# The norm between the second tree and the second graph layer waits for its gathered rows tile by tile

## What is computed

```python
x = x + _L0_ffn_ref(_layernorm(x, axis=-1)[None], ...)[0]   # ends with: return y + _fff(y, f_nw, ..., gelu)
xn = _layernorm(x, axis=-1)
x = x + _L1_gnn_ref(xn, edge_index, L1_gnn_W, L1_gnn_b) + _L1_mix_ref(xn[None], ...)[0]
```

## Time and profile before

| | |
|---|---|
| three runs | 2998.49, 2992.94 and 2996.53 us, median 2996.53 us |
| the profiled execution, its own time | 2996.26 us |
| the span that its trace covers | 2994.4 us |
| PE busy | 2788.4 us, 93% of the span |
| DVE, POOL, ACT busy | 1264.0, 790.9 and 582.8 us |

### The profile page before, as it was taken

One profiled execution on the slowest core, in us unless ns is written; L12 is line 12 of the kernel. 1 busy time (PEld: TensorE's weight loads), 2 busy tenths in 40 slices (PEclk: granted clock), 3 DMA queues, 4 the chain that ended last, 5 costly groups with the idle time before them and its releaser, 6 DMA issues.

```text
span 2994.4 us, 44272 instructions
## 1 busy us (share of the span) xinstructions
PE 2788.4 (93%) x15119; PEld 2273.6 (76%) x15120; DVE 1264.0 (42%) x1884; ACT 582.8 (19%) x784; POOL 790.9 (26%) x585
## 2 busy tenths in 40 slices
PE   7999999999999999989899999989969999888998
PEld 5679977799999999886667766667658879876444
DVE  8515699463323333374444434232443115233422
ACT  2222245321121221210111011101012212121110
POOL 0777699143322223221310001000013223310000
PEclk9999999999999999999899999989979999989999
DMA  5222212312211111330798988116931211111675
GB/s 201 64 79 72 61 53 89 89 49 68 67 44 53 43 43 57 128 146 35 267 346 293 335 279 312 52 54 220 318 110 36 72 62 50 57 51 44 212 250 196
DMA packets 104522, 378.54 MB, mean 126 GB/s; under 512 B 17672, under 2 KB 18353, under 8 KB 102965
## 3 DMA queue, kind: packets, MB, share of 16 engines
q1 hardware_dynamic: 83520, 301.25, 28.9%
q0 software_dynamic: 18560, 56.97, 6.3%
q10 hardware_dynamic: 2294, 18.27, 1.6%
HBM read 344.51 MB, written 31.75 MB: 126 GB/s over the span
## 4 chain that ended last, share of the span: by engine, by line
PE 76%; DVE 8%; issue 7%; DVEq 5%; DMA 2%; ACT 2%; POOL 0%; ACTq 0%; SPq 0%
PE pair L890 74%; DVE big L2226 2%; DVEq L2213 2%; PE pair L935 1%; DVE asum L2375 1%; ACT big L1625 1%; DVEq L2242 1%; DMA ring<-in_tree_w 1%; DMA ring<-in_wts 0%; DVEq L2076 0%; PE pair L1047 0%; DVE big L1927 0%; DVE rstd L2077 0%; DVE mu L2077 0%; DMA big<-xn_spill 0%
## 5 line engine op out<-in xcount | busy, mean ns | idle before, releaser
L890 PEld LDWEIGHTS pair<-big,ring 128*128 128x128 f32 x3200 | 451.9, 194 | 148.5 <-issue 81.8
L890 PE MATMUL pair<-big,ring 128*128 (+1 forms) x3200 | 539.2, 321 | 22.5 <-issue 10.0
L890 PE MATMUL pair<-mean_high,low 128*128 128x314 f32 x1280 | 290.8, 309 | 0.0
L890 PE MATMUL pair<-ring,hid_plan_heads 128*125 128x512 f32 x576 | 275.2, 601 | 14.9 <-DVE big L2226 14.3
L703 POOL DMA_INDIRECT edge_records<-big x160 | 208.9, 1305 | 110.3 <-issue 58.8
L890 PEld LDWEIGHTS pair<-mean_high,low 128*128 128x128 f32 x1280 | 215.0, 191 | 0.0
L744 POOL TENSOR_TENSOR low<-ring,high_tmp_a 128x1024 fp32r<-128x1024 f32 x36 | 97.0, 2695 | 428.6 <-ACT high_tmp_a L1705 428.6
L2226 DVE TENSOR_TENSOR big<-pair,big 125x1024 f32 x144 | 176.2, 1223 | 28.9 <-PE pair L890 20.7
L890 PE MATMUL pair<-ring,big 128*128 128x512 f32 x384 | 172.8, 606 | 8.2 <-DVE big L2792 8.2
L890 PE MATMUL pair<-big 125*128 125x128 f32 (+9 forms) x830 | 158.0, 344 | 13.2 <-ACT big L1515 2.6
L890 PEld LDWEIGHTS pair<-ring,hid_plan_heads 128*125 128x125 f32 x576 | 96.7, 188 | 93.8 <-issue 70.2
(11 more groups left out here) (488 smaller groups left out, 4826.2 us busy)
## 6 DMA issues: line engine op xcount, KB each, us to landing
ring<-in_tree_w SPq DMA_DIRECT2D x288, 512.0 KB
ring<-in_wts SPq DMA_DIRECT2D x276, 512.0 KB
counts_spill<-big POOLq DMA_DIRECT2D x1, 5349.1 KB, 29.0
big<-in_x_rows SPq DMA_DIRECT2D x5, 512.0 KB, 8.8
xn_rows_spill<-big POOLq DMA_DIRECT2D x1, 2560.0 KB, 8.5
edge_records<-big POOLq DMA_INDIRECT x160
big<-xn_rows_spill POOLq DMA_DIRECT2D x1, 2560.0 KB, 10.7
sorted_out_q<-big POOLq DMA_DIRECT2D x5, 512.0 KB, 5.6
```

The source lines that it names most:

```text
L890: ins = pe.matmul(o, lhsT, rhs, start=start, stop=stop)
```

## The change

The f tree's gathers no longer share a semaphore: each tile has its own, `tile_back[t]`. The wait at the head of the norm is now for the five stores (`out_stored["f"]`), and in the loop over tiles the addition of tile t waits for the gather of tile t alone.

```diff
-        rows_back = {f: sem(f"rows_back_{f}") for f in "qkvf"}
+        rows_back = {f: sem(f"rows_back_{f}") for f in "qkv"}
+        tile_back = [sem(f"tile_back{t}") for t in range(NT)]
...
-                    ).then_inc(rows_back[f], 16)
+                    ).then_inc(tile_back[t] if f == "f" else rows_back[f], 16)
...
                 if name == "ln2":
-                    v.wait_ge(rows_back["f"], 16 * NT)
+                    v.wait_ge(out_stored["f"], 16 * NT)
...
                     if name == "ln2":
+                        v.wait_ge(tile_back[t], 16)
                         j = JOB[f"ln2_in{t}"]
                         v.tensor_tensor(rows(t), ps[SLOT[j]][0:T, :], tok(b)[:, t, :],
                                         ALU.add).then_inc(psum_free[SLOT[j]], 1)
```

## The result

The changed kernel takes 2989.44 us, the median of 20 runs (2984.32 to 2997.22), beside 2995.52 us for the kernel before, 20 runs as well (2989.37 to 3003.24). That is 6.08 us less; the ratio is 0.998 with a 95% interval of 0.9972 to 0.9989. A second series of the same kernel, on another chip, gave 0.9984 (0.9974 to 0.9994); two of its twelve executions, 3305.37 and 7581.14 us, were far slower than the rest and are left out of its figures. So it is faster, by about as much as the forecast, 7.2 us, or a little less.

A forecast was written before the change was run, and what follows sets the result against it. PE was taken as the bound, busy 93% of the span, with an exposed gather wait before the norm. 7.31 us less 0.1 gave 7.2 us off 2996.53, so 2989.3 us; range 2985.5 to 2993.8 us.

The forecast's parts named there:

- The exposed wait and its size: Before the norm, DVE idles 11.08 us for the last gather; starting on tile 0 brings its first addition 7.31 us forward.
- What the start hangs on: Norm's first addition starts once tile 0 has landed, read from packets as 2191.1 to 2191.25 us; start taken as 2191.45.
- The signs: Expected in the changed trace: first addition 4.1 to 4.5 us after POOL's first gather, aggregation 24.9 us after it, not 32.1.
- the prediction's own limit of 6 us: Forecast counts as wrong if the stretch from first gather to the aggregation's first matmul shrinks by less than 6 us.
- Padding and POOL: Padding's 0.30 us leaves the path; DVE's earlier work beside POOL's gathers costs 0 to 0.3 us, taken as 0.1.
- Later tiles: In the norm, tiles 1 to 4 land before their additions, tile 1 almost 1 us early; cost taken as 0.
- The rival of a lagging DMA engine: Tile 1 lands late and holds the norm's second addition up to 0.8 us; gain 6.4 to 7.2 us; chance 10%.
- the other estimate: Skill's formula for a GpSimd-issued DMA: tile 0 lands 3.2 us after issue, gain about 8.3 us; not adopted.
- late clock: PE's clock rises late at the aggregation, 3.2 us at half speed; 1.6 us less gain, 2990.9 us; chance 10%.
- Slower than before: Behind the norm, over four of some eight slow-clock stretches last twice as long, erasing the gain; 2997.8 us; chance 5%.
- no effect: Tiles do not land one by one or DVE's start stays tied to all five gathers; 2996.5 us; chance 5%.
- The bound of 0.2%: Whole kernel: a measurement tells 0.2%, 6.0 us, from no change; faster 65%, within 31%, slower 4%.

The follow-up runs named there:

- padding late: Changed kernel, but the norm's padding waits for tile 0's gather instead of the stores; 2988.17 us beside 2997.58 us for the kernel before, ratio 0.997.
- added work of two SBUF inputs: Changed kernel plus four unused DVE additions with both inputs in SBUF, behind the residual's additions, beside POOL's gathers; one execution, 2988.84 us.
- residual early: Changed kernel with six of the eight residual additions moved ahead into the tree's last three steps; 2989.00 us beside 2996.46 us before, ratio 0.9976.
- added work of one SBUF input: Changed kernel plus one unused 4.07 us DVE reciprocal with a single SBUF input, behind the residual's additions, beside POOL's gathers; one execution, 2984.62 us.
- PE filled: Changed kernel with PE turning each of the first three tiles back three times in the norm; 2990.16 us beside 2996.46 us before, ratio 0.9978.

## Why the prediction was right, and where it was off

**The exposed wait and its size.** Right. The shift of the first addition was put at 7.31 us less 0.1; 7.20 us were measured (17.32 to 10.12), and 7.15 us at the aggregation. Counting sixteen small packets as the landing of a tile held: sixteen of them stand just ahead of the first addition here too.

**What the start hangs on.** Missed, and the sum did not need it. The sum took tile 0's landing from the packets of the trace and is right whatever held the gather. The signs took it from the start of POOL's first gather: the addition was to come 4.1 to 4.5 us behind it, and it was 5.21 us; from that gather to the aggregation 25.82 us were measured, not 24.9. In the profile of before, the stores landed 5.22 us after the last was issued, so the gather was held by the residual's additions for less than 0.1 us (1.03 us, beside 0.99 to 1.01 us where nothing held the first gather). In other executions the stores land sooner, the gather starts sooner, and the hold makes up the difference. So its start is a poor mark to count from: in the second series the stretch from the first gather to the aggregation is 26.51 us, 5.6 us less than before, and by the prediction's own limit of 6 us the forecast would have been wrong there, although the gain counted from the last tree addition is 7.02 us. Its other sign, a span that does not shrink, did appear in the profile, and came from the tree's later end. The rows showed this kind of hold; I looked for it at the padding and the norm, and not at the instructions that were already there.

**Padding and POOL.** The padding was put at 0.30 us; with the padding late it takes 0.29 us of the path. The 0.1 us that the prediction took off for POOL beside DVE's new work did not show: the padding ran beside a gather that the residual's additions held anyway, and the four later gathers took 0.94 to 0.98 us, as before.

**Later tiles.** Right: tile 1 is there 0.8 us ahead of its use (the prediction had almost 1 us), and additions 1 to 4 keep their pace. The rival of a lagging DMA engine, and with it the 6.5 us that I derived from the remark on two slower engines in the Trainium skill ("DMA: Bandwidth & Descriptors", Latency and other measured facts), did not come about: tile 1 was 2.4 us behind tile 0. Nor did the other estimate, a landing 3.2 us behind the issue and a gain of 8.3 us: a first gather that nothing held took 4.2 us to its landing beside the added work of two SBUF inputs, and 4.4 us with the residual early.

**Clock.** The term that was mis-sized, in its chance above all. I gave a late clock 10% and 1.6 us. Among the profiles in which the norm starts on tile 0 and PE's order is unchanged but for the fill, it was late in four (the changed kernel twice, padding late, added work of two SBUF inputs), by 1.7 to 2.2 us, and in time in three (added work of one SBUF input, PE filled, residual early). Where the norm starts later it was in time in all three profiles, before included. If it is late in half of the executions, at 1.9 us, the mean gain is 7.15 - 1 = 6.2 us, near the 6.08 us between the medians; the half is an assumption from these few profiles, so this is a possible account of the missing microsecond and not a measured one. The prediction's "4.2 us of transposes" ahead of the aggregation are 3.57 us of transposes and 0.65 us of waiting, and they are the same in the changed kernel, with a late clock, as before, with one in time, so they do not tell which it will be. Whether the change itself makes a late clock more frequent, or three profiles against seven are chance, stays open.

**Slower than before, and no effect.** Both fell. DVE's wait shrank from 11.08 to 3.69 us, and from the next weight block to the end the program took 718.82 us against 719.70 us, at a mean granted clock of 0.95 in both.

**The bound of 0.2%.** I gave 65% to more than that and 31% to within it. The median's 6.08 us are 0.203%, the second series' ratio is 0.16% off 1: both are at the line, and a late clock in some of the executions would put them there.

## What to carry to other kernels

When one instruction waits for a batch of transfers and then works through it piece by piece, the batch's last landing can be traded for its first; the gain is the distance between the two, provided each piece lands faster than it is used (2.4 against 3.07 us here), and it can be counted beforehand from the packets. Look also for what the consumer's consumer could start early: PE's first block needed only the tiles already scaled, and taking them one by one gave 5.6 us more. And compare profiles from an event that both share, since here the changed kernel's profiled execution was the longer one by 0.96 us. Take an event that the wait in question cannot move: the end of the last tree addition served, the start of the first gather did not.

## What was not expected of the hardware

A gather on POOL that is issued while DVE runs the residual's additions, with both inputs in SBUF, ends 0.85 to 0.87 us after the last of them, in each of the ten profiles in which they overlapped so, whether it was issued 0.17 us or 1.61 us before their end. It is not held by a reciprocal of 4.07 us with one SBUF input, nor by an addition that begins 0.06 us after it. Nor do the same additions hold a plain DMA: POOL issued the last store right behind their begin in every profile, and it took 0.53 us (2188.22 in the changed kernel, beside the additions from 2188.01), as the other stores did.

The Trainium skill ("SBUF — State Buffer", SBUF: two separate sides) describes an exclusive lock that goes to whoever starts first, that two SBUF inputs are enough to take against GpSimd work that reads SBUF, and that makes the other wait for the whole instruction. The runs agree that two SBUF inputs are enough and that a gather which starts first is not held; the gather takes its row numbers from SBUF. They do not agree that the other always waits: DVE's addition that began 0.06 us into a gather took 1.23 us, as the one behind it. The place where the hold mattered was an existing instruction, not the one that the change moved.
